# Products of exponentials and values: a group's four column tiles in two visits instead of four

## The chip, the cores and the metric

The kernel runs on one NeuronCore of a Trainium2 chip. The metric is the device time of one execution in microseconds. The engines are TensorE (PE, its weight loads PEld), VectorE (DVE), ScalarE (ACT), GpSimd (POOL) and SyncE (SP), which here only issues DMAs.

## The reference

One transformer block over 16 batches of 512 tokens of 128 numbers, in float32: causal attention with 16 heads of 8 numbers each, projection, residual and layernorm, then an FFN whose weights are +1 or -1, residual and layernorm.

```python
qkv = hidden_states @ c_attn_w + c_attn_b            # x: (16, 512, 128)
scores = jnp.einsum('bhqd,bhkd->bhqk', q, k) / jnp.sqrt(jnp.float32(hd))
scores = jnp.where(causal[None, None], scores, mask_value)
attn = jax.nn.softmax(scores, axis=-1)               # heads 0 to 2: reweighted and normalised again
out = jnp.einsum('bhqk,bhkd->bhqd', attn, v)
x = _layernorm(x + out @ c_proj_w + c_proj_b)
h = s0 * (concat([x, -x]) @ W0); h = relu(h) * 2
h = s1 * (h @ W1); h = relu(h) * 2
x = _layernorm(x + s2 * (h @ W2))
```

## The kernel before, in words

One *pass* is one `iteration(n)` (L980 on TensorE; each engine has its own). There are passes for n = -2 to 17; those of n = 3 to 12 are a hardware loop with two passes in its body, the others are unrolled. A pass works on several batches at once: the largest scores of each row of batch n+1, scores, exponentials and most of the value products of batch n, the last group's value products, the projection and the first layernorm of batch n-1, most of the FFN of batch n-2, and q and k of batch n+2.

A pass has four groups g of four heads, and each group ten steps t; (2, 3) is group 2, step 3. In each step TensorE does `max_scores` (products L827 and L829 into `max_ps`, a ring of three banks), then `scores` (L850 into `score_ps`, two banks). VectorE takes the maximum of a step (`take_max`: L645, L648 and L649, or L652), and ScalarE the exponential into `e` (L527). Keys are cut into four tiles of 128, and as the attention is causal, key tile kt needs only the query columns from 128 kt on: 512, 384, 256 and 128 columns for kt = 0, 1, 2, 3. Steps 0 to 3 of a group make tile 0 of its four heads, steps 4 to 7 tiles 1 and 3, steps 8 and 9 tile 2.

GpSimd zeroes the future half of the diagonal blocks of `e` (`mask`, L423, select L436), in three parts of a group: k = 0 for tile 0 (after exponential 4 of the group), k = 1 for tiles 1 and 3 (after the eighth), k = 2 for tile 2 (after the tenth). Each part raises `masked` by one. Its program is a fixed list (from L454): the masks stand between the low halves of the FFN's inputs (L443), the residual's bias (L464), the two splits of q and k (L418, L420), and the power operations of the layernorms (L448, then L451). The second split, `split_qk(2)`, stands right behind the power operation of the second layernorm, and the masks (2, 1) and (2, 2) stand behind that of the first.

The value products are `sums` (L862, matmul L883): `av_ps` holds four heads at once, each in 9 rows of a band of 32 partitions (eight numbers of v, and a one for the softmax's sum). One call makes one key tile of the four heads of a group: four float32 products, which the trace shows as eight matmuls of 9 columns of weights. Group g-1's products are made during group g, tile 0 at step 1, tile 1 at step 3, tile 3 at step 5 and tile 2 at step 7 (`SUM_STEPS`, L86, and L987 to L993); those of group 3 are made in group 0 of the next pass. At step 9 ScalarE copies `av_ps` out (`sums_out`, L530), which raises `av_out`. After the products of a step, `fill` gives TensorE the other work that is put down for it in `PLACES` (L45): among it the transposes of negmax at (0, 3) and (2, 3), FFN products at (0, 4), (0, 6), (0, 9), (1, 8) and (1, 9), the transposes of x_in at (0, 9), those of `ffn2` at (2, 2), the projection at (2, 6), the transposes of x1 at (3, 2) and the FFN's first layer from (3, 5). Two banks (`bank_ps`) serve all of these in turn.

The scores are made from a `stack` of bfloat16 parts of q and k, one for even and one for odd batches, each in two halves of eight heads. SyncE copies it from `parts` with nine DMAs a half (`stack_half`, L306, issue L313). `max_scores` of a batch waits for the first half at the start of a pass and for the second at its group 2. SyncE's program of a pass is, in this order: x_in, x_res, the negmax rows of batch n (half 1) and of batch n+1 (half 0; they are ready from step (2, 4) on), then, when both splits are done and batch n's scores of groups 0 and 1 are made, the first half of the stack of batch n+2; then the store of a finished batch, and when batch n's scores are all made, the second half. All go through one queue.

On VectorE step (2, 3) is `take_max`, then the sum of the FFN's output and residual (L753, which waits for the bank of `ffn2`), its statistics (L709), and mean and variance of the second layernorm (`layernorm_var`, L716 to L720). GpSimd's power operation waits for that, and `split_qk(2)` comes behind it.

Of the kernel before, what the change touches and what calls it, by code (L numbers as in the profile page):

```python
# [85 lines left out]
SUM_STEPS = (1, 3, 5, 7)  # L86
# [23 lines left out]
def block_kernel(nc, x, w_qkv, b_qkv, w_proj, b_proj, k0, k1, k2, s0, s1, s2, out):  # L110
    B, S, D = x.shape
    H, R = HEADS, D // HEADS
    P = 128
# [4 lines left out]
    G = 4  # L118
# [31 lines left out]
    with ExitStack() as ctx:  # L150
# [641 lines left out]
        def _(pe):  # L792
# [69 lines left out]
            def sums(b, g, kt, order):  # L862

                if order == 0:
                    pe.wait_ge(masked, b.times(3 * G, 3 * g + 1))
                    if g == 0:
                        pe.wait_ge(v_ready, b.times(1, 1))
                    if not (b.reg is None and b.c == 0 and g == 0):
                        pe.wait_ge(av_out, b.times(G, g))
                elif order == 1:  # L870
                    pe.wait_ge(masked, b.times(3 * G, 3 * g + 2))
                elif order == 3:
                    pe.wait_ge(masked, b.times(3 * G, 3 * g + 3))
                for j in range(G):
                    if kt == 0:
                        src = e[g % 2][:, j, :]
                    elif kt == 1:
                        src = e[g % 2][:, 4 + j, 0:3 * P]
                    elif kt == 3:
                        src = e[g % 2][:, 4 + j, 3 * P:S]  # L880
                    else:
                        src = e[g % 2][:, 8 + j // 2, 2 * P * (j % 2):2 * P * (j % 2) + 2 * P]
                    last = nc.tensor.matmul(av_ps[32 * j:32 * j + R + 1, P * kt:S],  # L883
                                            vaug[b.parity][:, kt, G * g + j, :], src,
                                            start=(order == 0), stop=(order == 3))
                if order == 3:
                    last.then_inc(summed, 1)
# [92 lines left out]
            def iteration(n):  # L980
                for g in range(G):
                    for t in range(STEPS):
# [4 lines left out]
                        if t in SUM_STEPS:  # L987
                            order = SUM_STEPS.index(t)
                            kt = (0, 1, 3, 2)[order]
                            if g == 0 and live(n + -1):  # L990
                                sums(n + -1, 3, kt, order)
                            if g > 0 and live(n):
                                sums(n, g - 1, kt, order)  # L993
# [27 lines left out]
```

## Time and profile before

| | |
|---|---|
| median of 3 runs | 1182.85 us (1182.3 to 1182.94) |
| span of the profiled execution, first to last instruction | 1183.4 us |
| TensorE busy | 923.2 us (78%) |
| VectorE busy | 705.5 us (60%) |
| ScalarE busy | 603.0 us (51%) |
| GpSimd busy | 455.0 us (38%) |
| `sums` matmuls (L883) | 2048, 199.0 us busy |
| chain that ended last | PE 54%, DMA 24%, issues of SyncE 11%, DVE 5%, ACT 4% |

The profile has no time of its own for the profiled execution but the span, which is 0.55 us above the median of the runs. Times of the trace are us from the first instruction. Busy shares are averages over stages with different limits; matmuls overlap, so a matmul's time is longer than its distance from the next one's start. A row of a timeline may stand for several instructions (x8); its time is then from the first start to the last end. In brackets stand the idle time of the engine just before, and what ended it. The granted clock (PEclk) is a share of 2.4 GHz.

### The profile page before, as it was taken

What the parts mean: (1) busy time and instruction counts of PE and PEld (TensorE: products, weight loads), DVE (VectorE), ACT (ScalarE), POOL (GpSimd) and SP (SyncE); (2) the same over time, 40 slices, a digit from 0 to 9 for tenths busy, and PEclk for the clock granted to TensorE, in tenths of its full rate; (3) what the DMA queues carried; (4) which work ended last, traced back from release to release, by engine and by line L of the source; (5) the groups of instructions that cost most, each with busy time, mean ns of one, the idle gap of its engine ahead of it and who ended that gap; (6) DMA issues with size and microseconds to landing.
All of it is one profiled execution on the core that took longest, in us unless ns stands there. A gap on an engine that the chain in (4) does not pass through costs nothing.

```text
span 1183.4 us, 20987 instructions
## 1 busy us (share of the span) xinstructions
PE 923.2 (78%) x6852; PEld 507.9 (43%) x6852; DVE 705.5 (60%) x1757; ACT 603.0 (51%) x1106; POOL 455.0 (38%) x508
## 2 busy tenths in 40 slices
PE   1154668889796969799797969697897969798875
PEld 0032333445453536455453535364454536364443
DVE  7154365848475665758475756657484756667234
ACT  0110353737374655747374656557373746556733
POOL 7010131434343443525343434435244434434550
PEclk9976797989898989989898989899898989899997
DMA  1524333251506151342416061433316060500000
GB/s 38 58 32 53 38 40 62 35 66 24 86 8 80 24 74 39 44 66 33 79 15 89 9 88 23 61 49 44 68 27 81 11 89 14 85 16 21 19 1 18
DMA packets 65773, 53.42 MB, mean 45 GB/s; under 512 B 4225, under 2 KB 63618, under 8 KB 65666
## 3 DMA queue, kind: packets, MB, share of 16 engines
q1 hardware_dynamic: 65666, 51.99, 31.0%
q8 instruction: 68, 1.11, 0.4%
q14 instruction: 39, 0.32, 0.1%
HBM read 9.24 MB, written 4.19 MB: 11 GB/s over the span
## 4 chain that ended last, share of the span: by engine, by line
PE 54%; DMA 24%; SPq 11%; DVE 5%; ACT 4%; issue 2%; POOL 1%; ACTq 0%; POOLq 0%; DVEq 0%
DMA stack<-parts 12%; DMA x_in<-in_L_attn_hidden_states 11%; SPq L313 11%; PE av_ps L883 10%; PE max_ps L827 10%; PE score_ps L850 9%; PE bank_ps L810 5%; PE bank_ps L910 4%; PE bank_ps L911 4%; PE max_ps L829 3%; PE bank_ps L956 3%; PE bank_ps L925 1%; PE bank_ps L926 1%; PE bank_ps L968 1%; ACT e L527 1%
## 5 line engine op out<-in xcount | busy, mean ns | idle before, releaser
L527 ACT ACTIVATE e<-score_ps 128x512 f32<-128x512 f32 x640 | 368.9, 598 | 357.1 <-PE score_ps L850 356.7
L827 PE MATMUL max_ps<-stack 96*128 96x512 bf16 (+3 forms) x1024 | 286.9, 321 | 164.8 <-DMA stack<-parts 140.5
L645 DVE TENSOR_REDUCE negmax<-max_ps 128x1 f32<-128x512 f32 x256 | 172.6, 687 | 230.4 <-PE max_ps L829 228.7
L436 POOL TENSOR_SCALAR_AFFINE_SELECT e<-e 128x512 f32<-128x512 f32 x256 | 161.8, 647 | 327.1 <-ACT e L527 327.1
L850 PE MATMUL score_ps<-stack 99*128 99x512 bf16 (+3 forms) x1024 | 255.7, 312 | 7.4 <-ACT e L527 7.1
L827 PEld LDWEIGHTS max_ps<-stack 96*128 96x128 bf16 x1024 | 103.2, 101 | 341.4 <-issue 158.9
L443 POOL TENSOR_TENSOR h_lo<-full,h_hi 128x512 fp32r<-128x512 f32 x120 | 153.3, 1278 | 211.9 <-DVE h_hi L725 211.2
L829 PE MATMUL max_ps<-ident_bf,future_bf 128*128 128x128 bf16 x1024 | 200.9, 228 | 0.0
L883 PE MATMUL av_ps<-e,vaug 128*9 128x512 f32 (+3 forms) x2048 | 199.0, 462 | 2.3 <-ACT avT L534 2.1
L648 DVE TENSOR_REDUCE negmax<-max_ps 128x1 f32<-128x384 f32 x256 | 140.5, 549 | 74.3 <-PE max_ps L829 74.2
L519 ACT ACTIVATE full<-bank_ps,scales 128x512 f32<-128x512 f32 x128 | 86.5, 688 | 90.5 <-PE bank_ps L911 88.9
L725 DVE CAST h_hi<-full 128x512 fp32r<-128x512 f32 x128 | 79.8, 624 | 61.0 <-ACT full L519 60.9
L829 PEld LDWEIGHTS max_ps<-ident_bf,future_bf 128*128 128x128 bf16 x1024 | 104.7, 102 | 24.0 <-issue 17.4
L850 PEld LDWEIGHTS score_ps<-stack 99*128 99x128 bf16 x1024 | 87.1, 101 | 59.6 <-ACT e L527 20.3
L910 PE MATMUL bank_ps<-h_hi,w 128*128 128x512 f32 x256 | 106.1, 414 | 0.6 <-DVE h_lo L730 0.3
L652 DVE TENSOR_REDUCE negmax<-max_ps 128x2 f32<-128x512 f32 x128 | 84.7, 684 | 35.2 <-PE max_ps L829 35.2
L911 PE MATMUL bank_ps<-h_lo,w 128*128 128x512 f32 x256 | 101.7, 397 | 0.0
L448 POOL TENSOR_TENSOR rstd<-var_eps,minus_half 128x4 f32<-128x4 f32 x32 | 32.5, 1015 | 119.4 <-DVE var_eps L720 119.4
L649 DVE TENSOR_REDUCE negmax<-max_ps 128x1 f32<-128x128 f32 x256 | 71.2, 278 | 0.0
L883 PEld LDWEIGHTS av_ps<-e,vaug 128*9 128x9 f32 x2048 | 30.8, 89 | 69.6 <-issue 64.9
L910 PEld LDWEIGHTS bank_ps<-h_hi,w 128*128 128x128 f32 x256 | 48.7, 190 | 15.3 <-issue 1.5
L418 POOL TENSOR_TENSOR qk<-qk,parts 128x1024 f32<-128x1024 f32 x15 | 32.0, 2135 | 58.3 <-ACT qk L519 58.3
(92 smaller groups left out, 1014.0 us busy)
## 6 DMA issues: line engine op xcount, KB each, us to landing
stack<-parts SPq DMA_DIRECT2D x288, 128.0 KB
x_in<-in_L_attn_hidden_states SPq DMA_DIRECT2D x16, 256.0 KB, 15.4
x_res<-in_L_attn_hidden_states SPq DMA_DIRECT2D x16, 256.0 KB, 13.7
out_x<-res SPq DMA_DIRECT2D x16, 256.0 KB, 16.1
stack<-negmaxT SPq DMA_DIRECT2D x32, 24.0 KB
e<-in_L_ffn_k SPq DMA_DIRECT2D x1, 256.0 KB, 3.3
wc<-in_L_attn_c_attn_w SPq DMA_DIRECT2D x1, 192.0 KB
e<-in_L_ffn_k SPq DMA_DIRECT2D x1, 128.0 KB, 3.2
```

What stands on the lines that cost most here:

```text
L313: sp.dma_start(stack[b.parity][row:row + R, HALF * half:HALF * half + HALF, :, :], src).then_inc(stacked[half], 16)
L436: last = nc.gpsimd.affine_select(out=ap, in_=ap, compare_op=ALU.is_ge, fill=0.0, base=0, pattern=[[0, 4], [1, P]], channel_multiplier=-1)
L443: nc.gpsimd.tensor_tensor(h_lo[layer][:, m, :], full[:, full_slot(b, k), :], h_hi[layer][:, m, :].bitcast(F32), ALU.subtract).then_inc(spl ...
L527: nc.scalar.activation(e[g % 2][:, t, :], score_ps[:, t % 2, :], ACT.Exp, scale=SCALE).then_inc(exped, 1)
L645: ins = nc.vector.reduce_max(negmax[:, half, 3, h + t:h + t + 1], buf, AX.X, negate=True)
L648: nc.vector.reduce_max(negmax[:, half, 2, i:i + 1], buf[:, 0:3 * P], AX.X, negate=True)
L827: nc.tensor.matmul(out_ap[:, col:col + width], st[0:QK_ROWS, h, 0, P * qt:P * qt + P], st[0:QK_ROWS, h, 1, 0:width], start=True, stop=False)
L829: return nc.tensor.matmul(out_ap[:, col + width - P:col + width], future_bf[:], ident_bf[:], start=False, stop=True)
L850: return nc.tensor.matmul(out_ap[:, col:col + width], st[0:ALL_ROWS, h, 1, P * kt:P * kt + P], st[0:ALL_ROWS, h, 0, P * kt:S], start=True, ...
L883: last = nc.tensor.matmul(av_ps[32 * j:32 * j + R + 1, P * kt:S], vaug[b.parity][:, kt, G * g + j, :], src, start=(order == 0), stop=(orde ...
L910: nc.tensor.matmul(bank, w, hi, start=(i == 0), stop=False)
L911: last = nc.tensor.matmul(bank, w, lo, start=False, stop=(i == len(pairs) - 1))
```

## The change

A group's value products are made in two visits. At step 2 tile 0 and then tile 3 (512 and 128 columns), at step 6 tile 1 and then tile 2 (384 and 256 columns). The first visit waits for `masked` of the parts k = 0 and k = 1 together, the second for k = 2. The first product of the group opens the accumulation, tile 2 closes it, and the last matmul of the second visit raises `summed`. Products, operands and columns are the same.

```diff
-SUM_STEPS = (1, 3, 5, 7)
+VISITS = (2, 6)
...
-            def sums(b, g, kt, order):
-
-                if order == 0:
-                    pe.wait_ge(masked, b.times(3 * G, 3 * g + 1))
+            def sums(b, g, visit):
+
+                if visit == 0:
+                    pe.wait_ge(masked, b.times(3 * G, 3 * g + 2))
                     if g == 0:
                         pe.wait_ge(v_ready, b.times(1, 1))
                     if not (b.reg is None and b.c == 0 and g == 0):
                         pe.wait_ge(av_out, b.times(G, g))
-                elif order == 1:
-                    pe.wait_ge(masked, b.times(3 * G, 3 * g + 2))
-                elif order == 3:
+                else:
                     pe.wait_ge(masked, b.times(3 * G, 3 * g + 3))
...
+                for kt in ((0, 3), (1, 2))[visit]:
+                    for j in range(G):
...
+                        last = nc.tensor.matmul(av_ps[32 * j:32 * j + R + 1, P * kt:S],
+                                                vaug[b.parity][:, kt, G * g + j, :], src,
+                                                start=(kt == 0), stop=(kt == 2))
+                if visit == 1:
                     last.then_inc(summed, 1)
...
-                        if t in SUM_STEPS:
-                            order = SUM_STEPS.index(t)
-                            kt = (0, 1, 3, 2)[order]
+                        if t in VISITS:
                             if g == 0 and live(n + -1):
-                                sums(n + -1, 3, kt, order)
+                                sums(n + -1, 3, VISITS.index(t))
                             if g > 0 and live(n):
-                                sums(n, g - 1, kt, order)
+                                sums(n, g - 1, VISITS.index(t))
                         fill(n, g, t)
```

## Rows read from the trace of the kernel before

**Rows 1.** Waits of TensorE: who waited for whom, us in total, times, longest.

```profile
PE max_ps L827 <- DMA stack<-parts: 140.5, 14, 26.0
```

**Rows 2.** Timeline of TensorE at a pass's start: start us, us, work [idle before <- releaser].

```profile
571.53 0.61 PE L827 MATMUL max_ps<-stack 96*128 96x512 bf16 x1 [8.73 <-DMA stack<-parts]
```

**Rows 3.** Chain of work that ended last, end of that pass: start us, us, what.

```profile
620.35 15.94 DMA stack<-parts
...
636.41 0.60 PE max_ps L827
```

**Rows 4.** Timeline of SyncE's DMA issues in that pass.

```profile
614.91 6.06 SPq L313 DMA_DIRECT2D stack<-parts  x9
```

**Rows 5.** Timeline of GpSimd ahead of those issues.

```profile
611.37 1.02 POOL L448 TENSOR_TENSOR rstd<-var_eps,minus_half 128x4 f32<-128x4 f32 x1 [4.58 <-DVE var_eps L720]
...
612.62 2.13 POOL L420 TENSOR_TENSOR parts<-qk,parts 128x1024 bf16<-128x1024 f32 x1
```

**Rows 6.** Timeline of VectorE ahead of that.

```profile
608.94 0.68 DVE L753 TENSOR_TENSOR res<-bank_ps,x 128x512 f32<-128x512 f32 x1
...
611.12 0.17 DVE L720 TENSOR_SCALAR var_eps<-moments 128x4 f32<-128x4 f32 x1
```

**Rows 7.** Timeline of TensorE in group 2, with two visits.

```profile
605.13 0.38 PE L850 MATMUL score_ps<-stack 99*128 99x512 bf16 x1
...
605.35 0.38 PE L827 MATMUL max_ps<-stack 96*128 96x512 bf16 x1
...
605.63 0.38 PE L850 MATMUL score_ps<-stack 99*128 99x512 bf16 x1
...
605.93 1.05 PE L883 MATMUL av_ps<-e,vaug 128*9 128x512 f32 x8
...
606.91 0.39 PE L827 MATMUL max_ps<-stack 96*128 96x512 bf16 x1
...
611.34 0.41 PE L883 MATMUL av_ps<-e,vaug 128*9 128x128 f32 x8
...
611.68 0.34 PE L827 MATMUL max_ps<-stack 96*128 96x384 bf16 x1
```

**Rows 8.** Timeline of TensorE's weight loads, same stretch.

```profile
605.93 0.12 PEld L883 LDWEIGHTS av_ps<-e,vaug 128*9 128x9 f32 x8 [0.27 <-issue]
```

**Rows 9.** Timeline of TensorE, two visits that stand together, last batch.

```profile
1129.59 1.05 PE L883 MATMUL av_ps<-e,vaug 128*9 128x512 f32 x8 [1.21 <-ACT avT L534]
...
1130.58 0.83 PE L883 MATMUL av_ps<-e,vaug 128*9 128x384 f32 x8
```

**Rows 10.** Timeline of GpSimd beside them.

```profile
1129.12 1.40 POOL L436 TENSOR_SCALAR_AFFINE_SELECT e<-e 128x512 f32<-128x512 f32 x2
```

**Rows 11.** Timeline of TensorE: transposes of x_in at step (0, 9), three passes.

```profile
136.00 1.12 PE L810 MATMUL bank_ps<-ident,x_in 128*128 128x128 f32 x4 [10.97 <-DMA x_in<-in_L_attn_hidden_states]
...
525.26 0.60 PE L810 MATMUL bank_ps<-ident,x_in 128*128 128x128 f32 x4
...
918.57 0.66 PE L810 MATMUL bank_ps<-ident,x_in 128*128 128x128 f32 x4 [0.23 <-DMA x_in<-in_L_attn_hidden_states]
```

**Rows 12.** Chain of work that ended last, pass from 242.42.

```profile
242.04 20.29 DMA x_in<-in_L_attn_hidden_states
```

**Rows 13.** Timeline of SyncE: issue of x_in in the pass from 505.86.

```profile
506.73 1.48 SPq L329 DMA_DIRECT2D x_in<-in_L_attn_hidden_states  x1
```

**Rows 14.** DMA issues in 504 to 510 us: KB each, us from issue to landing.

```profile
x_in<-in_L_attn_hidden_states SPq DMA_DIRECT2D x1, 256.0 KB, 18.4
```

**Rows 15.** Busy time by stretch (columns: engines in order, PEclk, DMA share, GB/s).

```profile
1072.00:1076.00 4.00, 3.67 (x28) 1.28 (x29) 2.78 (x5) 3.86 (x9) 1.83 (x5) 1.00 0.34 93
```

**Rows 16.** The same for the first 6 us of passes; PEclk is third from the end.

```profile
180.46:186.46 6.00, 6.00 (x24) 1.62 (x28) 2.92 (x8) 1.79 (x3) 0.00 (x0) 0.51 0.67 96
...
964.91:970.91 6.00, 6.00 (x37) 2.04 (x38) 3.10 (x8) 2.29 (x4) 0.55 (x1) 0.74 0.65 110
...
1027.31:1033.31 6.00, 6.00 (x24) 1.63 (x28) 2.92 (x8) 1.91 (x4) 0.00 (x0) 0.53 0.65 115
```

More of the change, by code:

```diff
@@ L869, in sums @@
                         pe.wait_ge(av_out, b.times(G, g))
-                elif order == 1:
-                    pe.wait_ge(masked, b.times(3 * G, 3 * g + 2))
-                elif order == 3:
+                else:
                     pe.wait_ge(masked, b.times(3 * G, 3 * g + 3))
[L874 to L886, printed above, removed]
+                for kt in ((0, 3), (1, 2))[visit]:
+                    for j in range(G):
+                        if kt == 0:
+                            src = e[g % 2][:, j, :]
+                        elif kt == 1:
+                            src = e[g % 2][:, 4 + j, 0:3 * P]
+                        elif kt == 3:
+                            src = e[g % 2][:, 4 + j, 3 * P:S]
+                        else:
+                            src = e[g % 2][:, 8 + j // 2, 2 * P * (j % 2):2 * P * (j % 2) + 2 * P]
+                        last = nc.tensor.matmul(av_ps[32 * j:32 * j + R + 1, P * kt:S],
+                                                vaug[b.parity][:, kt, G * g + j, :], src,
+                                                start=(kt == 0), stop=(kt == 2))
+                if visit == 1:
                     last.then_inc(summed, 1)
```

## The prediction

> **What bounds the kernel now.** The list of waits comes first, since it says what stops TensorE: the max products of L827 waited 14 times for the copies `stack<-parts`, 140.5 us in all [rows 1]. These waits stand at the start of a pass (one value of n, one batch in each stage): at 571.53 the first matmul of a pass came after 8.73 us of nothing [rows 2]. So the end of a pass on TensorE doesn't set the time; the copies do, and I follow them back. The chain of waits shows the landing 15.94 us after the last of nine issues [rows 3]; SyncE began these at 614.91 [rows 4], and the next pass started 21.5 us later, at 636.41 (620.35 + 15.94 is 636.3). SyncE began when GpSimd's second split, 612.62 + 2.13, was done; GpSimd runs in a fixed order, and ahead of that split stands the power operation at 611.37, which idled 4.58 us for VectorE's `var_eps` [rows 5]. VectorE got there through the sum into `res` at 608.94, without a pause to 611.12 + 0.17 [rows 6], and that sum comes behind the max of step (2, 3). So the loop that sets the time is: start of a pass, TensorE's work up to the max of step (2, 3), then some 28 us of VectorE, GpSimd, SyncE and DMA, then the next start. What TensorE does in the rest of groups 2 and 3 ends in the 8.73 us of idleness.
>
> **What one visit costs.** I call the run of products with `vaug` at one step a visit. From the first matmul of a visit to the next one of another kind it took 0.98 us at 512 columns (605.93 to 606.91) and 0.34 at 128 (611.34 to 611.68) [rows 7]. The 0.64 between them are 384 columns, so 0.213 for each 128; 0.98 less four of them leaves 0.13 that doesn't grow with the columns. Ahead of a visit stands another gap: a score product of 512 columns is followed by the next matmul after 0.22 us (605.13 to 605.35), but by a visit after 0.30 (605.63 to 605.93) [rows 7]. A visit thus costs 0.13 + 0.08 = 0.21 us beside its columns. That is the price of changing over to products that fill 9 of the array's columns in four places and back. The Trainium skill, "TensorEngine Tiling (Array Packing)", section Tiling Modes, says that a change of tiling mode drains the TensorEngine; the fixed 0.21 agrees.
>
> **The change part by part.** *Removed:* two of four visits in each group, 0.42 us a group. *Joined:* tile 0 with tile 3 (512 + 128 columns) at step 2, tile 1 with tile 2 (384 + 256) at step 6; products, columns and sizes stay. I cost the join inside a visit at nothing: in a visit all eight weight loads stand in 0.12 us at its head, while its products run on for 1 us [rows 8], so the second four products find their weights loaded. The one place where two visits stand together now shows a gap: first one from 1129.59, second from 1130.58, where 512 columns end after 0.85, at 1130.44, so 0.14 [rows 9]. But the second waited there for the mask that GpSimd ended at 1129.12 + 1.40 = 1130.52 [rows 10]. I take 0 and keep 0.14 as the other end.
>
> *Moved, critical part.* Up to the max of (2, 3) a pass has nine visits now (four in groups 0 and 1, one in group 2), and will have five: 4 x 0.21 = 0.84 us less. But tile 3 of group 2's first visit moves ahead of it: 0.21 more. Net 0.63 us a pass.
>
> *Moved, hidden part.* In group 2 the visit of step 6 goes ahead of the projection, so VectorE's, GpSimd's and ScalarE's norm work comes about 0.2 us later against step (2, 0). The waits: the first visit now needs the second mask and not only the first. Ahead of (0, 2), (1, 2) and (2, 2) GpSimd has nothing but its own lows and masks to do first, and that mask is long made. Ahead of (3, 2) it stands behind the power operation of the first norm, and TensorE will wait, about 0.5 us by my estimate, with the transposes of x1 and the FFN's first layer queued behind. I cost that at nothing in all passes that end in the stall, and in the one that doesn't below. The wait on `av_out` gets a step more of time; it was short anyway.
>
> *How many passes.* Fourteen starts hang on this loop. In seven of them group 0's share, two visits or 0.42 us, is not to be had, for the transposes of x_in at (0, 9) then wait for its landing, which follows the start and not TensorE. Five waited already (the first 10.97 us, the last 0.23) [rows 11]; in the pass from 242.42 the chain of waits runs over x_in, 242.04 + 20.29 [rows 12]; in the pass from 505.86 it landed at 506.73 + 18.4 = 525.13 [rows 13, 14], 0.13 ahead of the transposes at 525.26 [rows 11]. These seven give 0.21, the other seven 0.63: 1.5 + 4.4 = 5.9 us.
>
> *The end.* The pass from 1027.31 has no stall behind it. Groups 0 and 1 give 0.84. Groups 2 and 3 don't: around 1072 to 1076 ScalarE is busy 3.86 of 4 us [rows 15], and the mask wait at (3, 2) eats what the fewer visits give; I take 0.8 in all. The last batch's group 3, in the pass after next, has its visits with the FFN's products between them and tile 1 moves into the later one: 0.2 more. Sum: 5.9 + 0.8 - 0.2 = 6.5 us.
>
> *The clock.* After each stall TensorE works at 1.2 GHz for a while, then at 2.4: in the first 6 us of a pass the granted clock averaged 0.51 in the first, 0.74 at best and 0.53 in the last of the fourteen [rows 16]. As the clock is 0.5 and then 1, the slow part is (1 - clock) x 12: 5.9, 3.1 and 5.6 us; its mean over the fourteen is 4.4. It costs half its length. The change shifts where a pass meets the step and says nothing of the direction; I take the middle of the ends, 4.5, for the new mean: 14 x 0.1 / 2 = 0.7 us lost. A mean 0.7 us to either side would be 5 us.
>
> So 5.8 us: 1183.4 becomes 1177.6. The median of the runs shown is 1182.85, 0.55 below the profiled execution's span; less 5.8 it is 1177.0.
>
> **The rivals.**
> *All visits are on the path* (0.06). 64 groups x 0.42 = 27 us, 1156. For it: TensorE is the busiest engine. Against it: the stall [rows 1, 2] takes what half the visits give.
> *The gain is swallowed, within 0.2%* (0.21). Either x_in or the slow clock takes it (all fourteen passes give 0.21 and the slow part grows by 0.3 us: 2.9 + 0.6 - 2.1 = 1.4 us), or the joins cost a weight load each: five joins stand on the loop, 5 x 0.09 = 0.45, leaving 0.18 a pass, 14 x 0.18 = 2.5 less what x_in hides. About 1181. For it: x_in's margins [rows 11] and the spread of the clock [rows 16]. The 0.09 is the load's part of the 0.12 in which eight of them overlap [rows 8]. The Trainium skill, "TensorE: Matmul & The Clock Gate", section Part 3, says that weight loads overlap running matmuls only where the row groups differ. All products here use all rows, so by that rule each join would stand open for a load and this rival would hold. The trace speaks against it, as the second four loads of a visit stand at its head.
> *The joins cost what the visits cost* (0.13, the slower one). If the 0.21 belongs to the change of tile and width, not to the change of kind of product, nothing is removed; the 0.14 at 1130.44 [rows 9] would be a sign of it. Then each pass has tile 3's product and the join ahead of (2, 3): 0.21 + 0.21 = 0.42 more, 14 x 0.42 = 5.9 us, 1189. It decides from a join of 0.63 / 5 = 0.13 us on. Against it stands the mask that ended 0.06 us before the second visit [rows 10].
>
> **How the numbers follow.** Measurements of this kernel tell about 0.2%, 2.4 us, from no change. My forecast, 1177, has 0.60; swallowed 0.21; slower 0.13; all visits 0.06. Faster is 0.66, the same 0.21, slower 0.13. The range: below, fourteen full passes (8.8 + 0.6 us, 1173.5) and a slightly shorter slow part, 1172; above, the swallowed gain and a mean slow part 0.5 us longer (14 x 0.25 = 3.5), 1184.5. That leaves out the slower rival's full price and the fastest.
>
> **What would show it.** Right: 1,024 score and max products as before, and visits of about 1.19 us (640 columns x 0.213 / 128 + 0.13) with no gap between their second and third four products; from the start of a pass to SyncE's first of nine issues 0.2 to 0.6 us less than 43.4 (571.53 to 614.91) [rows 2, 4]; the stalls still there, about 8 us each; a short wait for GpSimd's mask at (3, 2). Wrong: a visit of 1.3 us or more (the joins cost), a stall that shrinks by several us (another loop), or more or longer waits for x_in at (0, 9).

## The result, and the profile after

The changed kernel takes 1196.72 us (median of 16 runs, 1186.5 to 1199.4), beside 1185.16 us for the kernel before (16 runs): a ratio of 1.009, 95% interval 1.0073 to 1.0107. It is 11.6 us slower, 10.7 by the ratio. The forecast was 1177.0 with a range up to 1184.5, so it was wrong in sign and outside its range. The profiled execution has a span of 1197.7 us, against 1183.4; it is the longest of the sixteen (1199.4, 2.7 above their median), so the 14.3 us between the two spans are more than what the change costs.

Two lines of the page, the busy time of TensorE and the group of the products with `vaug`:

```profile
PE 920.3 (77%) x6852; PEld 531.4 (44%) x6852; DVE 711.0 (59%) x1757; ACT 605.1 (51%) x1106; POOL 452.7 (38%) x508
...
L882 PE MATMUL av_ps<-e,vaug 128*9 128x512 f32 (+3 forms) x2048 | 179.7, 472 | 8.9 <-POOL e L436 8.9
```

The same 2048 products are there; they took 199.0 us before and 179.7 now. The change does what it says. The engine that it relieves gains, and the kernel loses.

The waits (who waited for whom: us in total, times, longest), answering to [rows 1]:

```profile
PE max_ps L827 <- DMA stack<-parts: 120.2, 15, 26.7
...
DVE negmax L645 <- issue: 25.9, 3, 8.7
...
PE bank_ps L909 <- DVE x_lo L730: 15.1, 16, 2.0
...
PE bank_ps L893 <- DVE res L753: 10.1, 13, 0.8
PE av_ps L882 <- POOL e L436: 8.9, 16, 1.9
```

The wait for the copies shrank from 140.5 to 120.2 us. "issue" is time in which an engine waited for nothing that the profile shows: VectorE has three such pauses, 25.9 us in all and 8.7 at the longest, which the kernel before does not list; it lists two of TensorE (20.1 us, at back edges of the loop, where an engine jumps back to the start of the loop's body; more of them below), and the changed kernel one (10.4). The other three lines are TensorE's, in groups 2 and 3: the wait for `x_lo` was 2.0 us in all before, those for `res` and for the mask are new.

One visit (timeline of TensorE, then of its weight loads), answering to [rows 7, 8]:

```profile
531.82 1.26 PE L882 MATMUL av_ps<-e,vaug 128*9 128x512 f32 x16
533.02 0.77 PE L810 MATMUL bank_ps<-ident,avT 128*128 128x128 f32 x5
```

```profile
531.82 0.12 PEld L882 LDWEIGHTS av_ps<-e,vaug 128*9 128x9 f32 x8 [0.27 <-issue]
532.26 0.11 PEld L882 LDWEIGHTS av_ps<-e,vaug 128*9 128x9 f32 x4 [0.32 <-issue]
532.69 0.11 PEld L882 LDWEIGHTS av_ps<-e,vaug 128*9 128x9 f32 x4 [0.32 <-issue]
```

The visit of 640 columns takes 533.02 - 531.82 = 1.20 us, forecast 1.19, and the loads of the second four products stand at 532.26 and 532.69, within the running ones. The join costs nothing.

A pass of the changed kernel (start at 645.77, to be laid beside the pass from 571.53), answering to [rows 2, 4, 5, 6]; timelines of TensorE, VectorE, GpSimd and SyncE:

```profile
645.77 0.60 PE L827 MATMUL max_ps<-stack 96*128 96x512 bf16 x1 [6.87 <-DMA stack<-parts]
```

```profile
683.34 0.68 DVE L753 TENSOR_TENSOR res<-bank_ps,x 128x512 f32<-128x512 f32 x1
...
685.52 0.16 DVE L720 TENSOR_SCALAR var_eps<-moments 128x4 f32<-128x4 f32 x1
```

```profile
685.76 1.02 POOL L448 TENSOR_TENSOR rstd<-var_eps,minus_half 128x4 f32<-128x4 f32 x1 [4.45 <-DVE var_eps L720]
...
687.01 2.13 POOL L420 TENSOR_TENSOR parts<-qk,parts 128x1024 bf16<-128x1024 f32 x1
```

```profile
689.28 6.03 SPq L313 DMA_DIRECT2D stack<-parts  x9
```

From the start of the pass to SyncE's issue: 689.28 - 645.77 = 43.51 us, before 614.91 - 571.53 = 43.38. The slow part of the clock was 4.82 us in this pass and 3.99 in that one; with half of each taken off (it costs half its length), 41.10 against 41.38. So 0.28 us of the forecast 0.63 are there.

### Where the 14.3 us between the two profiles lie

The start of a pass is TensorE's first max product, as at 571.53 before:

| stretch | before | after | more |
|---|---|---|---|
| to the start of pass n = 2 | 242.42 | 245.64 | 3.2 |
| n = 2 to 12, the last ten of them in the loop | 722.49 | 729.21 | 6.7 |
| n = 13 | 62.40 | 62.58 | 0.2 |
| last stretch, to the end | 156.1 | 160.3 | 4.2 |

The first 3.2 are not the change's: they come with a wait for `x_in` of 5.82 us where the profile of before had 2.94, and kernels below with four visits in all groups show 5.34 to 5.92. The 6.7 us lie in four passes, those from 376.77 (1.9 us longer), 575.81 (5.1), 711.35 (0.9) and 842.11 (1.6), 9.5 together; the other seven are 2.8 us shorter. The loop body holds two passes, so there are four back edges in the ten. The pass from 376.77 stands right before one and the other three right behind one (eight of the ten passes stand beside a back edge, so that alone is no proof).

The pass from 376.77 is TensorE's. Its next start isn't released by the copies (timeline of TensorE, after; at 440.86 before the idle time was 9.92 us, also "issue"):

```profile
445.34 0.61 PE L827 MATMUL max_ps<-stack 96*128 96x512 bf16 x1 [10.37 <-issue]
```

TensorE's work of this pass ended 58.2 us after its start in place of 56.7, and a pause of its own at the back edge follows: 25.4 us from SyncE's issue to the next start (23.1 before), where passes that wait for the copies have 21.2 to 22.4.

The other three are VectorE's. VectorE at one back edge, before and after (timelines of VectorE):

```profile
564.08 1.45 DVE L725 CAST h_hi<-full 128x512 fp32r<-128x512 f32 x1 [0.55 <-ACT full L519]
574.03 0.69 DVE L645 TENSOR_REDUCE negmax<-max_ps 128x1 f32<-128x512 f32 x1 [8.50 <-PE max_ps L829]
```

```profile
571.43 1.01 DVE L725 CAST h_hi<-full 128x512 fp32r<-128x512 f32 x1 [0.62 <-ACT full L519]
581.15 0.69 DVE L645 TENSOR_REDUCE negmax<-max_ps 128x1 f32<-128x512 f32 x1 [8.72 <-issue]
```

In a pass without a back edge ahead of it VectorE's first reduction comes 0.75 us after the start. Here it came 2.50 us after it already before (574.03 - 571.53), and comes 5.34 after it now (581.15 - 575.81). The idle time is the same, 8.50 and 8.72: it isn't a wait for TensorE, whatever the first row says, but a standstill of much the same length each time that begins at the end of VectorE's pass. Of that end only 6.0 us were left to the next start before, and 3.4 now (572.44 to 575.81). What sticks out holds TensorE, which has three banks for its max products. Its own waits for VectorE are short here, 0.78 and 0.63 us; but at the start of this pass it stays at 1.2 GHz for 13.3 us, where it was 4.0 before, and half of the difference is 4.7 of the pass's 5.1 us. The loss in this pass is paid almost whole through the clock. (In late_wait, below, where VectorE alone was made late, three passes have 8.6 to 12.5 us of it.)

### The profile page after: what moved, and what is told of

Its sections match the earlier page's. It is cut to its first block, busy times and chain, and to the rows that moved or that the text cites. A ratio compares the mean times of both kernels' runs of the same rounds, so it can differ in the third digit from the quotient of the medians.

```text
span 1197.7 us, 20957 instructions
## 1 busy us (share of the span) xinstructions
PE 920.3 (77%) x6852; PEld 531.4 (44%) x6852; DVE 711.0 (59%) x1757; ACT 605.1 (51%) x1106; POOL 452.7 (38%) x508
## 4 chain that ended last, share of the span: by engine, by line
PE 47%; DMA 19%; issue 9%; DVE 9%; SPq 9%; ACT 3%; POOL 3%; DVEq 0%; POOLq 0%; ACTq 0%
DMA x_in<-in_L_attn_hidden_states 10%; DMA stack<-parts 9%; PE av_ps L882 9%; SPq L313 8%; PE max_ps L827 8%; PE score_ps L850 7%; PE bank_ps L909 5%; PE bank_ps L910 4%; PE bank_ps L810 4%; PE max_ps L829 3%; PE bank_ps L955 3%; DVE negmax L645 1%; POOL e L436 1%; DVE negmax_parts L665 1%; PE bank_ps L924 1%
## 5 line engine op out<-in xcount | busy, mean ns | idle before, releaser
L827 PE MATMUL max_ps<-stack 96*128 96x512 bf16 (+3 forms) x1024 | 290.0, 324 | 144.5 <-DMA stack<-parts 120.2
L850 PE MATMUL score_ps<-stack 99*128 99x512 bf16 (+3 forms) x1024 | 258.7, 315 | 15.9 <-ACT e L527 14.9
L882 PE MATMUL av_ps<-e,vaug 128*9 128x512 f32 (+3 forms) x2048 | 179.7, 472 | 8.9 <-POOL e L436 8.9
L725 DVE CAST h_hi<-full 128x512 fp32r<-128x512 f32 x128 | 76.9, 601 | 62.9 <-ACT full L519 62.9
L882 PEld LDWEIGHTS av_ps<-e,vaug 128*9 128x9 f32 x2048 | 45.4, 93 | 124.7 <-issue 118.7
## 6 DMA issues: line engine op xcount, KB each, us to landing
x_res<-in_L_attn_hidden_states SPq DMA_DIRECT2D x16, 256.0 KB, 14.3
```

Source lines behind the costliest of these rows:

```text
L827: nc.tensor.matmul(out_ap[:, col:col + width], st[0:QK_ROWS, h, 0, P * qt:P * qt + P], st[0:QK_ROWS, h, 1, 0:width], start=True, stop=False)
L850: return nc.tensor.matmul(out_ap[:, col:col + width], st[0:ALL_ROWS, h, 1, P * kt:P * kt + P], st[0:ALL_ROWS, h, 0, P * kt:S], start=True, ...
```

## The experiments

All ratios are against the kernel before, measured beside each kernel, with their 95% intervals. "Written out" means `UNROLL = 10`: the ten passes of the loop stand one behind the other, with no back edge between them.

### Half of the change

```diff
-VISITS = (2, 6)
+PLAN = ({2: (0, 3), 6: (1, 2)}, {2: (0, 3), 6: (1, 2)},
+        {1: (0,), 3: (1,), 5: (3,), 7: (2,)}, {1: (0,), 3: (1,), 5: (3,), 7: (2,)})
```

A line of `PLAN` is a group: at which step which column tiles are multiplied. merged_01 has two visits in groups 0 and 1 and four in 2 and 3; merged_23 the other way round.

> Two visits only in groups 0 and 1 of a pass, the old four in groups 2 and 3. Theory A (the loss comes from groups 2 and 3, whose work now ends later, so that the idle stretch at the end of a pass no longer covers VectorE's standstill of 8.2 to 8.7 us at every second pass): from a pass's start to SyncE's nine issues 0.4 to 0.8 us less than before, group 2 to the end of a pass unchanged at 23.3 us, VectorE's first work of a pass at most 2.5 us behind TensorE's; in all 4 to 9 us faster than the kernel before, about 1178. Theory B (joining visits costs wherever it is done, by starving the other engines): slower than before, by about half of the change's 11.5 us, 1190.

Measured 1185.95, ratio 1.0014 (0.9996 to 1.0031). No gain: the 4 to 9 us were missed.

> Two visits only in groups 2 and 3, the old four in groups 0 and 1. Theory A: the whole loss without the gain: group 2 to the end of a pass 25 to 27 us in place of 23.3, VectorE 3 to 5 us late at three starts or more, 12 to 18 us slower than the kernel before, about 1199. Theory B: about half of the change's loss, 1190.

Measured 1201.19, ratio 1.0142 (1.0114 to 1.0169). The loss lies in groups 2 and 3, those that the prediction called hidden. The halves don't add up: with groups 2 and 3 merged the kernel is 16.8 us slower by the ratio, and merging groups 0 and 1 as well gives 6 of them back (10.7 for the whole change), while on its own it gives nothing. So two explanations are needed, and neither half is free of the other.

### The back edge

```diff
-UNROLL = 2
+UNROLL = 10
```

> The kernel before with all ten passes of the loop in one body (UNROLL 10), so that no engine jumps back. Theory A: no standstill of 8 us or more on VectorE or 10 us on TensorE ahead of a pass that is not a wait; the two passes of 66.6 and 67.1 us shrink to about 65.3, 3 us faster, 1182. Theory B says nothing of it: no change.

Measured 1177.63, ratio 0.9948 (0.9928 to 0.9968): about twice the 3 us expected.

> The changed kernel with all ten passes in one body. Theory A: the passes of 68.6, 70.0 and 67.3 us shrink to about 65.4, and the difference to the kernel before with the same body falls from 11.5 us to 3 to 6, which is what the second start (x_in) and the end of the program make; about 1186. Theory B: the difference to the kernel before with the same body stays near 11.

Measured 1182.24, ratio 0.9992 (0.9977 to 1.0007). Without back edges the change costs 4.6 us and not 11.6, so 7 us of its loss would need the back edge; against the later run of the same written-out kernel (before_u10_b below, 0.9925) it costs 7.9, and 3 or 4 would. In the profiles the passes n = 2 to 12 take 711.5 us with two visits, and with four 715.3 here and 711.2 in before_u10_b, so no gain in them is shown. The last stretch, which no wait for copies ends, is 6.1 us longer (160.6 against 154.5, and 154.4 in before_u10_b).

That is still a comparison of kernels that differ in much. So VectorE's end was moved by itself, in the kernel before:

```diff
+            def late_iteration(n):
+                iteration(n)
+                if n.reg is not None:
+                    for k in range(5):
+                        nc.vector.reduce_max(scratch[:, k:k + 1], wc[:], AX.X, negate=True)
```

> The kernel before with five idle max reductions of a constant tile (384 columns each, about 2.2 us together) at the end of VectorE's work of each of the ten passes of the loop; nothing reads them, nothing else changes, four visits stay. Theory C (at the loop's back edge VectorE stands still for some 8.5 us counted from its last instruction, and only what is left of that when the copies land is seen): VectorE begins the four passes behind a back edge about 2 us later than now (now 0.9 to 2.5 us after the start of the pass), TensorE runs out of max banks there, and the kernel is 5 to 11 us slower, 1190 to 1196. Rival, the one my prediction rested on (whatever ends before the stall of 8 to 9 us is over is hidden): no change, within 2 us of the kernel before.

Measured 1187.26, ratio 1.0032 (1.0009 to 1.0055): less than the 5 us expected.

> The same five reductions, with the ten passes of the loop written out, so that no back edge is left between them. Theory C: VectorE still ends 5 us before the next start, so nothing is lost against the written-out kernel before (1177.6): 1176 to 1180. Rival (a later end of a pass costs by itself, whether or not there is a back edge): the loss of the first of these two runs comes again, 1183 to 1190.

Measured 1180.59, ratio 0.9955 (0.9933 to 0.9977), 0.6 us above the range, and by the ratio not to be told from 0.9948: hidden.

The standstill didn't move with the reductions (timeline of VectorE in late_vector; the pass starts at 569.95):

```profile
562.76 1.45 DVE L726 CAST h_hi<-full 128x512 fp32r<-128x512 f32 x1 [0.56 <-ACT full L520]
564.13 2.38 DVE L793 TENSOR_REDUCE scratch<-wc 128x1 f32<-128x384 f32 x5
572.98 0.69 DVE L646 TENSOR_REDUCE negmax<-max_ps 128x1 f32<-128x512 f32 x1 [6.47 <-issue]
```

The idle time fell to 6.47. From the last cast, the last instruction that had to wait, to the first reduction it is 10.2 us here, 9.95 before (574.03 - 564.08) and 9.72 in the changed kernel. Five instructions that wait for nothing seem to be passed on at once. My theory had the wrong starting point. These rows fit a standstill that counts from where the instruction stream reaches the back edge, not from where the datapath falls idle. The next pair makes the stream itself late:

```diff
-                        nc.vector.reduce_max(scratch[:, k:k + 1], wc[:], AX.X, negate=True)
+                        nc.vector.reduce_max(scratch[:, k:k + 1], wc[:], AX.X,
+                                             negate=True).then_inc(late, 1)
+                        dve.wait_ge(late, At(n.c - LOOP[0], n.reg).times(5, k + 1))
```

> The kernel before with the same five idle max reductions of a constant tile at the end of VectorE's work of each pass of the loop, but now each is waited for before the next instruction, so that VectorE's instruction stream, and not only its datapath, reaches the back edge about 2.5 us later. Theory C2 (the standstill counts from the last instruction that waits: 9.5 to 9.95 us from the issue of the last h_hi cast to the first reduction in seven of the eight kernels so far, 10.1 to 10.6 where the unwaited reductions stood in between): VectorE begins the passes behind a back edge at about 4.5 to 5.5 us after their start where it now begins at 2.5, idles 8.2 to 8.8 us by itself, and the kernel is 4 to 10 us slower, 1189 to 1195. Rival (VectorE's part in the back edge isn't what costs, TensorE's is): within 2 us of late_vector's 1187.

Measured 1201.7, ratio 1.0149 (1.0119 to 1.0178): 17.6 us more, beyond the 4 to 10 expected.

> The same waited reductions with the ten passes written out, no back edge between them. Theory C2: hidden behind the wait for the copies, 1177 to 1181, as with the unwaited ones (1180.6). Rival (a later end of VectorE costs by itself): 1184 and more.

Measured 1177.87, ratio 0.9948 (0.9922 to 0.9973): what before_u10 took. The same 2.89 us of idle reductions cost 17.6 us with the two-pass body and nothing without (timelines of VectorE and of TensorE in late_wait, pass from 574.62, then VectorE in late_wait_u10, pass from 567.98):

```profile
570.07 2.89 DVE L794 TENSOR_REDUCE scratch<-wc 128x1 f32<-128x384 f32 x5
582.45 0.69 DVE L647 TENSOR_REDUCE negmax<-max_ps 128x1 f32<-128x512 f32 x1 [9.49 <-issue]
```

```profile
583.20 0.61 PE L837 MATMUL max_ps<-stack 96*128 96x512 bf16 x1 [3.61 <-DVE negmax L647]
```

```profile
564.85 2.89 DVE L794 TENSOR_REDUCE scratch<-wc 128x1 f32<-128x384 f32 x5
568.80 0.69 DVE L647 TENSOR_REDUCE negmax<-max_ps 128x1 f32<-128x512 f32 x1 [1.06 <-PE max_ps L839]
```

VectorE begins 7.83 us late, TensorE's fourth max waits 3.61 us for it, and that pass lasts 72.3 us where 65 is usual (70.7 behind two other back edges). Nothing was changed on TensorE, so the rival that only TensorE's part of the back edge costs is out. Written out, the reductions end 0.24 us ahead of the start and the first max is read at 0.82. How late VectorE began behind the four back edges, and what the kernels cost (us above the kernel before, from the ratio):

| kernel | VectorE's first reduction after the start | us more |
|---|---|---|
| k_ahead | 2.17, 2.02, 1.84, 0.75 | -4.4 |
| before | 0.98, 2.50, 2.40, 0.89 | 0 |
| merged_01 | 1.15, 2.57, 2.54, 0.75 | 1.7 |
| placed | 0.80, 2.13, 1.92, 0.86 | 2.2 |
| late_vector | 0.75, 3.03, 2.87, 2.88 | 3.8 |
| merged_012 | 1.74, 2.98, 3.12, 1.37 | 5.4 |
| changed | 0.75, 5.34, 3.70, 5.14 | 10.7 |
| merged_23 | 3.62, 3.48, 1.98, 3.40 | 16.8 |
| late_wait | 3.00, 7.83, 7.54, 7.31 | 17.6 |
| shift_3 | 3.39, 5.27, 3.62, 3.22 | 22.8 |

(placed, k_ahead and shift_3 are kernels of the next sections.) The order fits roughly, but for merged_23 and shift_3, which cost more than their lateness here says. In merged_23 two passes, those from 637.43 and 772.43, are ended by TensorE's own pauses (9.18 and 7.25 us, "issue") and not by the copies, and from its start to SyncE's issue a pass of the loop takes 44.3 us on average, against 43.6 before: tile 3 now stands ahead of (2, 3) with no visit less in groups 0 and 1, and the slow part of the clock is longer. I did not split its cost further.

The Trainium skill, "Runtime: NRT & Kernel Launch", section Instruction fetch mechanics, says that a taken branch whose target isn't in the pages at hand makes the engine wait for the fetch of the target. Here VectorE's idle time at a back edge was 8.2 to 9.6 us where nothing but the standstill filled it (7.7 and 7.8 in shift_3, 7.8 once in late_wait). The Trainium skill, "Advanced Engine Details and Errata", section Engine Queue Depths, gives VectorE a queue of 8, into which the five unwaited reductions fit. Both agree with these runs. The traces hold something more for the fetch: among the packets that their pages call "q14 instruction", one of 8 KB starts 2.1 to 3.6 us ahead of VectorE's first reduction at every one of the forty back edges of the ten kernels with a two-pass body, at 571.4 for the reduction at 574.03 before, and at 579.7 for the late one at 582.45 in late_wait. A whole run has only some forty packets of that queue. Which engine a packet serves the trace doesn't say, so the fetch is supported and not proven.

### Why groups 2 and 3 end late

In the changed kernel the pass from 645.77 (timeline of TensorE in group 3):

```profile
694.23 1.27 PE L882 MATMUL av_ps<-e,vaug 128*9 128x512 f32 x16 [0.51 <-POOL e L436]
695.43 0.66 PE L810 MATMUL bank_ps<-ident,x 128*128 128x128 f32 x4
...
698.57 0.50 PE L909 MATMUL bank_ps<-x_hi,w 128*128 128x512 f32 x1 [0.87 <-DVE x_lo L730]
```

The mask wait is the forecast one, 0.51 us. Behind it the transposes of x1 come late, and the FFN's first layer waits 0.87 us for `x_lo`, where two visits used to stand between them. These are not the only new pauses: TensorE also waits 0.7 to 0.8 us for `res` at (2, 3) and 0.7 to 0.8 us for VectorE's maximum at the head of group 3, in every pass of the loop, where TensorE in the kernel before has no wait of over 0.45 us anywhere in groups 1 to 3. One visit was moved behind those transposes:

```diff
-{2: (0, 3), 6: (1, 2)})     # group 3
+{3: (0, 3), 6: (1, 2)})
```

> The changed kernel with one visit moved by a step: the first visit of group 3 stands at step 3, behind the transposes of x1, and not at step 2, ahead of them. Theory D (the visit at (3, 2) delays those transposes by its 1.19 us and its mask wait, and then nothing is left to fill TensorE's wait for x_lo ahead of the FFN's first products): the mask wait at (3, 2) and the 0.9 us wait for x_lo go, the pass ends 1.3 to 2 us earlier on TensorE and VectorE, the back edges show less, and the kernel takes 1185 to 1192 instead of 1196.7. Rival E (the end of the pass is late because VectorE and ScalarE are behind in groups 2 and 3, whatever TensorE's order): the wait for x_lo only moves, 1194 to 1198.

Measured 1207.26, ratio 1.0193 (1.0161 to 1.0226). Theory D fell, and so did rival E: it is 10 us worse (timeline of TensorE, then busy time, clock and DMA of a stretch, PEclk third from the end):

```profile
692.45 1.12 PE L810 MATMUL bank_ps<-ident,x 128*128 128x128 f32 x4 [1.13 <-ACT x L545]
```

```profile
692.00:698.50 6.50, 6.05 (x34) 2.89 (x35) 2.61 (x6) 3.06 (x7) 1.38 (x2) 0.50 0.62 80
```

Moved away, the visit uncovers a wait of 1.13 us for the norm's output x, which in the changed kernel it had hidden; and within this pause the granted clock falls to 0.50 (1.2 GHz) and stays there through the 6.5 us of the row, in the middle of group 3. The changed kernel has the same in a smaller form:

```profile
558.44:561.84 3.40, 3.26 (x21) 1.41 (x22) 0.45 (x1) 1.69 (x4) 0.60 (x2) 0.50 0.66 100
```

Such a stretch, 3.4 us at 0.50, stands in six of its passes from 510.04 on (four of them in the loop), and in none of the loop's passes in the kernel before. The other six passes of the loop have the same pauses, to a few hundredths, and no such stretch, so the pauses go with the fall of the clock and don't settle it alone. So in these groups the visits seem to be filling: small work that covers TensorE's waits for ScalarE, GpSimd and VectorE. Which group it is:

> Two visits in groups 0, 1 and 2, four in group 3. Theory G (group 3's two visits carry the loss: in the changed kernel the first one is ahead of the transposes of x1, delays them by 1.2 us and waits for its mask, and the FFN's first products then wait for x_lo with nothing in between): about as merged_01, 1184 to 1188. Rival H (group 2's visits carry it, since with them the second transposes, the projection and all that VectorE does with it come later): 1192 to 1198.

Measured 1188.42, ratio 1.0046 (1.0024 to 1.0068), a little above Theory G's range.

> The same three groups with the ten passes of the loop written out. Theory G: 1173 to 1177, as merged_01_u10 (1176.0) or a little better by the end of the last batches. Rival H: 1180 to 1183, as with two visits everywhere (1182.2).

Measured 1180.49, ratio 0.9961 (0.9939 to 0.9983): at the low end of H's range by the time, and halfway between merged_01_u10 (0.9928) and after_u10 (0.9992) by the ratio. From merged_01 by way of merged_012 to the changed kernel the ratio grows by 0.0032 for group 2 and 0.0044 for group 3 (3.8 and 5.2 us) with the back edges, and by 0.0033 and 0.0031 (3.9 and 3.7 us) written out. So both groups cost, and neither theory holds alone. Then places against number, with three visits each:

```diff
-        {2: (0, 3), 6: (1, 2)}, {2: (0, 3), 6: (1, 2)})                 # groups 2, 3
+        {1: (0,), 3: (1,), 7: (3, 2)}, {1: (0,), 3: (1, 3), 7: (2,)})
```

> Two visits in groups 0 and 1 as in the changed kernel; three in group 2 (tile 0 at step 1, tile 1 at step 3, tiles 3 and 2 at step 7, behind the projection) and three in group 3 (tile 0 at step 1, tiles 1 and 3 at step 3, behind the transposes of x1, tile 2 at step 7). Twelve... ten visits a pass in place of sixteen. Theory P (places decide, not the number): the projection is 0.3 us earlier than in the kernel before, TensorE and VectorE end the pass no later, VectorE begins behind the back edges at 0.8 to 2.6 us, and the time is that of merged_01 or a little less, 1181 to 1186. Rival N (fewer visits mean more of VectorE's and ScalarE's lateness whatever their places): TensorE's waits for them grow, 1188 to 1194.

Measured 1187.76, ratio 1.0019 (0.9999 to 1.0039). VectorE begins at 0.80, 2.13, 1.92 and 0.86 us behind the back edges, a little earlier than before the change, and the loss is gone. The time is 1.8 us above theory P's range and 0.2 below rival N's. Ten visits a pass in place of sixteen, and nothing gained either.

> The same plan of visits with the ten passes of the loop written out. Theory P: 1172 to 1176. Rival N: 1178 to 1182.

Measured 1176.52, ratio 0.9923 (0.9896 to 0.995): half a microsecond above theory P's range, and what four visits take written out (0.9948 and 0.9925).

### Why groups 0 and 1 give nothing

> Two visits in groups 0 and 1, four in groups 2 and 3, and the ten passes of the loop written out. With four visits throughout that takes 1177.6, with two throughout 1182.2. Theory A (merging on the stretch that sets the time gives 0.3 to 0.6 us a pass, of which the slow clock and VectorE's lateness in group 2 take a part): 1172 to 1176. Rival F (from group 2 on VectorE sets the pace, so the gain of groups 0 and 1 is gone before SyncE issues): 1176 to 1179, with the time from the start of a pass to SyncE's issue unchanged at about 43.3 us.

Measured 1175.98, ratio 0.9928 (0.9899 to 0.9956); beside before_u10 that is too little to tell, so both were measured once more, side by side.

> Four visits in every group, the ten passes written out, beside the next kernel on one chip: about 1177.6 again (ratio 0.995).

Measured 1174.82, ratio 0.9925 (0.9898 to 0.9951).

> Two visits in groups 0 and 1, the ten passes written out. Theory A (the loop's period falls by 0.3 to 0.5 us with the time from a pass's start to SyncE's issue, as the profiles of 65.03 and 64.53 us say, and the last passes lose 1 to 2): 1 to 4 us less than the kernel beside it. Rival F (no gain: VectorE sets the pace from group 2 on): within 1 us of it.

Measured 1176.58, ratio 0.9927 (0.9902 to 0.9952). No gain even without back edges, as rival F has it, but its reason isn't in the traces. From a pass's start to SyncE's issue, with half of the slow part of the clock taken off, the two profiles with four visits have 41.34 and 41.36 us on average over the passes n = 3 to 13, and the two with merged_01's visits 40.98 and 41.01: 0.35 us of the forecast 0.63 are there in each pass. (With the two-pass body it is 41.51 and 41.12.) Two things take it back. The slow part is 0.1 to 0.5 us longer in these passes (0.65 with the two-pass body), and costs half of that. And the last stretch is 2.2 us longer in both (156.7 and 156.6 against 154.5 and 154.4; 159.0 against 156.1 with the two-pass body).

Where the rest of the 0.63 might go shows in GpSimd and VectorE at the head of group 2 in the changed kernel:

```profile
677.40 1.22 POOL L436 TENSOR_SCALAR_AFFINE_SELECT e<-e 128x512 f32<-128x512 f32 x2 [2.64 <-ACT e L527]
678.59 2.13 POOL L418 TENSOR_TENSOR qk<-qk,parts 128x1024 f32<-128x1024 f32 x1
```

```profile
679.98 0.78 DVE L665 CAST negmax_parts<-negmax 128x32 bf16<-128x32 f32 x1
```

A cast of 32 columns takes 0.78 us, where it takes 0.17 elsewhere, and ends (680.76) when GpSimd's split ends (680.72); before the change it took 0.30. The Trainium skill, "SBUF — State Buffer", section "SBUF: two separate sides", says that VectorE in its fast modes and GpSimd lock one port pair for a whole instruction. The rows agree, though they don't show in which mode the cast ran. GpSimd's split follows its mask, the mask ScalarE, and ScalarE the product for k at (1, 6), which in the changed kernel stands behind a visit:

```profile
673.16 1.26 PE L882 MATMUL av_ps<-e,vaug 128*9 128x384 f32 x16
674.35 1.12 PE L955 MATMUL bank_ps<-xT,wqk 128*128 128x512 f32 x2
```

So a chain of waits leads from TensorE's (1, 6) to VectorE's delayed cast. If it set the time, and not the max of (2, 3), the gain would be smaller. Ahead of (1, 6) three visits fewer save 0.63 us, but the 256 columns of tile 2 moved in front, 0.43: net 0.20, and 0.28 was measured. Moving that visit one step back, in the kernel placed, tests it:

```diff
-        {2: (0, 3), 6: (1, 2)},     # group 1
+        {2: (0, 3), 7: (1, 2)},
```

> placed_u10 with one visit moved: in group 1 tiles 1 and 2 at step 7 and not at step 6, so that the k product at (1, 6) no longer stands behind 640 columns. Theory K (the chain leaves TensorE at the k product: ScalarE's copies of k, GpSimd's mask, its split of 2.13 us, VectorE's first cast of negmax, which now takes 0.79 us because it ends with the split): the k product about 1.2 us earlier, the cast back at 0.2 to 0.4 us, SyncE's issue 0.4 to 0.5 us earlier in every pass, the period 64.2 instead of 64.6, 14 x 0.45 = 6 us less than placed_u10 (1176.5): 1169 to 1173. Rival M (my first chain, over the max of (2, 3)): the number of columns ahead of that max is the same, so nothing changes, 1175 to 1178.

Measured 1172.52, ratio 0.9886 (0.9859 to 0.9913).

> The same move with the two-pass body, beside placed (1187.8). Theory K: SyncE's issue comes 0.4 to 0.5 us earlier, but so does the next start against VectorE's standstill at the back edge, so that at two of the four back edges VectorE begins about 0.4 us later than in placed: 3 to 6 us less than placed, 1182 to 1185. Rival M: 1186 to 1189.

Measured 1182.5, ratio 0.9963 (0.9941 to 0.9985), 5 us less than placed (7 by the ratios) and 3 to 4 less than the kernel before. The total hits theory K, its place only half (k_ahead_u10, pass from 690.23; timelines of VectorE and TensorE):

```profile
724.49 0.17 DVE L665 CAST negmax_parts<-negmax 128x32 bf16<-128x32 f32 x1
...
725.95 0.69 DVE L645 TENSOR_REDUCE negmax<-max_ps 128x1 f32<-128x512 f32 x1 [0.37 <-PE max_ps L829]
```

```profile
717.57 1.13 PE L957 MATMUL bank_ps<-xT,wqk 128*128 128x512 f32 x2 [0.22 <-DVE attn L702]
```

The cast is back at 0.17 us, so the first link is shown. But the ten passes of the loop stay as long as in placed_u10 (64.58 and 64.54 us on average): the k product now waits for a bank that VectorE frees, and VectorE waits again for TensorE's max. So that this chain sets the loop's time is not shown. The gain lies in the passes n = 0 and 1, where VectorE's chain has no `res` yet: 64.02 became 62.12 us, and 62.50 became 60.44, 4.0 together. These two passes vary from profile to profile, but the two kernels with this move have the shortest of all (122.6 and 120.9 us together, the eighteen others 124.9 to 130.7).

## Why the prediction was wrong

- *The visit, its 0.21 us and the join at nothing*: right (1.20 us for 1.19; loads inside). TensorE's busy time fell, and the rivals about joins were empty.
- *"What TensorE does in the rest of groups 2 and 3 ends in the 8.73 us of idleness"*, costed at nothing: this is the step that failed. merged_23, with only these groups merged, loses 16.8 us, more than the whole change. The stall belonged to TensorE's wait for the copies alone. At a back edge VectorE needs 8.5 us of its own, of which the start left 6.0; the stretch was not slack for whatever makes VectorE late. The pair with waited reductions shows it (17.6 us with back edges, nothing without). TensorE has a pause of its own there too, and ended too late for it once (1.9 us in the pass from 376.77). The loss left by two doors, the back edges (3 to 7 us) and the last stretch (below). The prediction had named a stall that shrinks by several us as a sign of being wrong: TensorE's idle time ahead of the next start fell from 8.6 to 6.4 us on average over the passes n = 3 to 13. The trace of before had the sign: VectorE's idle time of 8.50 us ahead of a first reduction at 2.50 us, behind two of the four back edges.
- *The mask wait at (3, 2), about 0.5 us*: right in size (0.51), but its consequences were not followed: late transposes, 0.87 us for `x_lo`, and, in four of the loop's passes, 3.4 us of slow clock in mid-pass.
- *The critical part, 0.63 us a pass up to the max of (2, 3)*: mis-sized. 0.28 was measured in the pass shown, and 0.35 on average with groups 0 and 1 alone. The chain over the k product and the cast may hold the rest, but k_ahead_u10 took that link away and the loop's passes didn't get shorter, so the cause stays open.
- *The slow part of the clock at 4.5 us*: right, 4.4 us over twelve of the fourteen passes; the two behind late back edges had 13.3 and 6.5. They raise the mean to 5.2, so the clock lost 5.3 us where the sum took 0.7.
- *The end, 0.8 - 0.2 gained*: wrong sign. The last stretch lost 4.2 us (6.1 written out). The first 2.2 of the 6.1 come with groups 0 and 1 alone (merged_01_u10), for which the sum had a gain of 0.84; group 2 adds 1.5 and group 3 adds 2.4. There no wait for copies covers the later end of groups 2 and 3. And the first visit of the last batch's group 3, which is made in group 0 of the next pass, waited 1.89 us (2.20 in merged_01_u10_b) for the second mask, which tile 3 needs, where the first of four visits needs the first mask alone.
- *The slower rival* had the right sign for a cause that did not occur.

Left open: merged_23's share between back edges and why merging groups 0 and 1 gives back 6 us there, what holds the other half of the 0.63 us a pass, and how the last stretch's 4.2 us split between its waits.

## What to carry to other kernels

A stall on one engine is slack only for work that ends in that engine; ask of every engine that will now finish later what it has to do before the next start, a loop's back edge included. Small pieces of work that look like overhead may be what covers the waits between them: before merging them, list what each one stands in front of. Look at the last passes by themselves, where nothing hides a delay. And follow the chain back at every engine's first slow instruction, not only from the one with the longest wait.

## What the hardware showed that I had not expected

- A loop's back edge stops VectorE for 7.7 to 9.6 us, and TensorE, where its pause and not the copies ended last, for 9.2 to 11.4 us (7.25 once in merged_23, 6.4 and 6.8 in shift_3). It is seen only as far as it sticks out behind another wait. Writing ten passes out gave 0.52 to 0.75% by itself.
- Instructions that wait for nothing do not delay it: at the three back edges where VectorE came late, 2.38 us of them moved the first reduction by 0.3 to 0.8 us from the last cast, and 2.89 us of waited ones by 3.6 to 4.0 (13.7 us from the last cast and not 9.95). That is about 1 us more than the reductions themselves, which is not explained.
- VectorE's late start costs little by TensorE's waits (0.78 and 0.63 us in the pass from 575.81) and much by the clock (9.3 us more at 1.2 GHz).
- Within or just behind pauses of 0.5 to 1.2 us in the middle of a pass, the last of several, the granted clock fell to 1.2 GHz for 3.4 to 6.8 us in six of the changed kernel's passes and most of shift_3's; other passes with the same pauses kept 2.4 GHz.
